# Three rotating diagonal slots, separate spreads of queries and values, and rows split into halves once per group and turned by transfers, in an attention and mixture-of-experts kernel

## The reference

```python
def xattn(q, k, v):                       # q = layernorm(x), k = v = ctx; each (4096, 16 heads, 16)
    scores = einsum('sqd,skd->sqk', qh, kh) / sqrt(16)
    scores = where(tril(ones(16, 16)), scores, -1e18)
    return einsum('sqk,skd->sqd', softmax(scores), vh)
...
def ffn(x, gate_w, gate_b, w1, b1, w2, b2):
    top1 = argmax(x @ gate_w.T + gate_b)
    for e in range(8):
        h = relu(x @ w1[e].T + b1[e])     # 1024 hidden
        y = h @ w2[e].T + b2[e]
        out = out + where(top1 == e, y, 0)
...
x = x + xattn(layernorm(x), ctx, ctx)
x = x + ffn(layernorm(x), ...)
```

## Time and profile before

| | |
|---|---|
| median of 3 runs | 477.7 us (477.31 to 478.84) |
| span of the profiled execution | 492.6 us |
| PE busy, share of the span | 402.1 us, 82% |
| DVE busy | 346.3 us, 70% |
| ACT busy | 177.5 us, 36% |
| POOL busy | 208.7 us, 42% |
| chain that ended last, by engine | PE 55%, DMA 11%, SPq 9%, DVE 9%, issue 6%, POOL 5% |
| bytes moved by DMA | 69.39 MB |

### The profile page before, as it was taken

One profiled execution on the slowest core, in us unless ns is written; L12 is line 12 of the kernel. 1 busy time (PEld: TensorE's weight loads), 2 busy tenths in 40 slices (PEclk: granted clock), 3 DMA queues, 4 the chain that ended last, 5 costly groups with the idle time before them and its releaser, 6 DMA issues.

```text
span 492.6 us, 16316 instructions
## 1 busy us (share of the span) xinstructions
PE 402.1 (82%) x5967; PEld 338.3 (69%) x5967; DVE 346.3 (70%) x777; ACT 177.5 (36%) x317; POOL 208.7 (42%) x213
## 2 busy tenths in 40 slices
PE   0135868888888866897999999779999999999992
PEld 0025757887787765896887877557778877877871
DVE  7978969789945863477757877457666666766662
ACT  3343255542624221342434433224333333433420
POOL 8345374334673467523723242642333323233221
PEclk9999999999999999975699999889999999999998
DMA  8999578899685664377612232544333322222210
GB/s 282 414 305 218 135 170 241 212 259 260 160 220 119 152 167 107 106 173 181 207 45 67 68 76 81 185 131 155 90 68 77 77 62 62 69 60 61 84 31 0
DMA packets 105162, 69.39 MB, mean 141 GB/s; under 512 B 78077, under 2 KB 88190, under 8 KB 104576
## 3 DMA queue, kind: packets, MB, share of 16 engines
q1 hardware_dynamic: 75696, 56.67, 41.9%
q10 hardware_dynamic: 25984, 3.21, 4.6%
q0 software_dynamic: 3408, 8.46, 4.6%
HBM read 48.28 MB, written 12.57 MB: 124 GB/s over the span
## 4 chain that ended last, share of the span: by engine, by line
PE 55%; DMA 11%; SPq 9%; DVE 9%; issue 6%; POOL 5%; ACT 2%; ACTq 1%; another core or an unknown queue 1%; POOLq 0%; DVEq 0%
PE s_ps L1229 20%; SPq L305 8%; PE at_ps L1245 6%; DMA arena<-qv_hl 6%; PE pv_ps L1245 6%; PE pv_ps L1143 6%; PE s_ps L1111 3%; PE lg_ps L1171 3%; PE pv_ps L1246 3%; PE at_ps L1246 3%; POOL qv_hl L987 2%; PE tr_ps L1156 2%; DMA arena<-x 2%; PE st_ps L1196 2%; POOL k_hl L995 1%
## 5 line engine op out<-in xcount | busy, mean ns | idle before, releaser
L1229 PEld LDWEIGHTS s_ps<-arena 128*128 x1872 | 132.7, 99 | 52.2 <-issue 14.6
L1229 PE MATMUL s_ps<-arena 128*128 128x128 f16 x1872 | 158.6, 222 | 8.4 <-DVE arena L906 5.1
L915 DVE SCALAR_TENSOR_TENSOR arena<-arena,s_ps 128x512 f32<-128x512 f32 x78 | 53.6, 687 | 48.6 <-PE s_ps L1229 35.9
L1076 POOL DMA_INDIRECT result<-arena x39 | 38.8, 995 | 95.5 <-DVE arena L940 91.6
L1111 PEld LDWEIGHTS s_ps<-k_hl,arena 128*128 128x128 f16 x1536 | 54.3, 118 | 29.9 <-DMA arena<-qv_hl 22.1
L1111 PE MATMUL s_ps<-k_hl,arena 128*128 128x16 f16 x1536 | 54.7, 179 | 23.3 <-DMA arena<-qv_hl 19.3
L1143 PE MATMUL pv_ps<-a_hl,arena 128*128 128x16 f16 x1536 | 54.7, 179 | 19.7 <-DMA arena<-qv_hl 15.9
L1143 PEld LDWEIGHTS pv_ps<-a_hl,arena 128*128 128x128 f16 x1536 | 53.5, 118 | 22.8 <-DMA arena<-qv_hl 18.3
L1245 PE MATMUL at_ps<-arena,k_in 128*128 x160 | 60.9, 383 | 0.8 <-DVE k_hl L926 0.6
L1245 PE MATMUL pv_ps<-arena,x_in 128*128 x152 | 58.1, 383 | 0.1
L1069 POOL TENSOR_TENSOR arena<-arena 128x256 f32<-128x256 f32 x39 | 30.7, 786 | 60.7 <-DMA arena<-b 60.6
(11 more groups left out here) (143 smaller groups left out, 614.2 us busy)
## 6 DMA issues: line engine op xcount, KB each, us to landing
arena<-w SPq DMA_DIRECT2D x28, 512.0 KB, 6.1
arena<-sorted_rows SPq DMA_DIRECT2D x39, 130.0 KB, 2.4
arena<-b SPq DMA_DIRECT2D x39, 128.0 KB
arena<-qv_hl SPq DMA_DIRECT2D x70, 64.0 KB, 3.5
k_in<-k_t SPq DMA_DIRECT2D x16, 256.0 KB, 3.9
v_in<-v_t SPq DMA_DIRECT2D x16, 256.0 KB
arena<-x SPq DMA_DIRECT2D x4, 1024.0 KB, 12.1
o_sb<-x_r SPq DMA_DIRECT2D x16, 256.0 KB, 3.8
```

Of the source, the lines that this page charges most:

```text
L915: eng.scalar_tensor_tensor(out=h_in[:, c].rearrange("p (k t) -> p k t", t=P), in0=bias, scalar=W_SCALE, in1=h_ps[c][:].rearrange("p (k t) ...
L1076: eng.indirect_dma_start(out=out, out_offset=bass.IndirectOffsetOnAxis(ap=rows[:, r, :].bitcast(I32)[:, D + 2:D + 3], axis=0), in_=rows[:, ...
L1229: k = eng.matmul(o, weights_of(j, w + k_ * H + n * P, P), xt[:, j % 2, k_ * P:(k_ + 1) * P], start=k_ == 0 and w is HI_1 and xt is xt_hi, ...
```

## The change

1. **Three slots in rotation.** Block i uses slot i mod 3 for its queries and, once its scores are done, for its values. `spread_first_part` and the joint transfer go; each block has eight parts of queries (waiting for outputs of block i-3) and eight of values (waiting for scores of block i), half as large as the joint ones. Expert 7's late load waits for outputs of block 14 (`s_pv >= NC - 1`); the first fetch of rows waits for outputs of block 13.
2. **Rows split per group.** After a group's layer norm, ScalarE normalises its rows (8 activations), casts them to fp16 (2 copies), and GpSimd subtracts for the rests (2 operations). Both halves travel in the row: 516 floats for 260. The scatter waits for them. In the expert stage a transposing transfer (`dma_start_transpose`) brings 128 rows x 512 halves into `xt`, three buffers; the plain fetch brings the first 260 floats. Normalisation, transposes and split per tile go on ScalarE, TensorE and VectorE, and with them the bank `st_ps` there. The residual add waits for the fetch.
3. **Zeros.** A lane of their own on GpSimd; VectorE clears the first slot.
4. **Order.** The due times of all lanes stand in a table `TIMES`, in hundredths of a microsecond, and all are new; ScalarE's three parts are steps of their own. Expert tiles are due 5.28 us apart from 338.87 us on.
5. The buffer of GpSimd's DMA descriptors is set to 4096 bytes.

```diff
-    ROW = D + 4
+    FETCHED = D + 4
+    ROW = FETCHED + D
...
-        q_bd = diagonals[:, 2 * SLOT_BLOCKS:], diagonals[:, 0:SLOT_BLOCKS]
-        v_bd = [q_bd[0] if i == NC - 2 else diagonals[:, SLOT_BLOCKS:2 * SLOT_BLOCKS] for i in range(NC)]
+        SIDES = 3
+        diagonal = [diagonals[:, n * SLOT_BLOCKS:(n + 1) * SLOT_BLOCKS] for n in (1, 2, 0)]
...
+        xn1 = sb("xn1", [P, G // 2, D])
+        x1_hi, x1_lo = [pay[:, :, FETCHED:].bitcast(F16)[:, :, n * D:(n + 1) * D] for n in range(2)]
...
-        def spread_part(eng, i, n):
+        def spread_part(eng, i, n, halves_of):
             part, cols = slice(HD * n, HD * (n + 1)), slice(HEADS * n, HEADS * (n + 1))
-            at = slice(1 - i % 2, 3 - i % 2)
-            if i + 2 < NC:
-                to = diagonals[part, at.start * SLOT_BLOCKS:at.stop * SLOT_BLOCKS, cols]
-                eng.dma_start(to, qv_hl[part, at].rearrange("p s b c u a -> p (s b) c u a")).then_inc(s_bd[i % 2], 16)
-            else:
-                eng.dma_start(v_bd[i][part, :, cols], v_hl[part]).then_inc(s_bd[i % 2], 16)
+            eng.dma_start(diagonal[i % SIDES][part, :, cols], halves_of[part]).then_inc(s_bd[i % SIDES], 16)
...
                     if e == E - 1:
-                        sp.wait_ge(s_qk, NC)
+                        sp.wait_ge(s_pv, NC - 1)
...
+            def spread_queries():
+                for i in range(NC):
+                    yield
+                    if i < SIDES:
+                        sp.wait_ge(*((s_zero_0, 1), (s_zero, 1), (s_zero, 2))[i])
+                    else:
+                        sp.wait_ge(s_pv, i - SIDES + 1)
                     sp.wait_ge(s_q_hi, i + 1)
                     sp.wait_ge(s_q_lo, i + 1)
+                    for n in range(8 - LATER):
+                        spread_part(eng, i, n, q_hl[i % 2])
+
+            def spread_values():
+                for i in range(NC):
+                    yield
                     sp.wait_ge(s_v_hi, i + 1)
                     sp.wait_ge(s_v_lo, i + 1)
+                    sp.wait_ge(s_qk, i + 1)
                     for n in range(8 - LATER):
+                        spread_part(eng, i, n, v_hl)
...
-                    sp.wait_ge(s_pv, NC - 1)
+                    sp.wait_ge(s_pv, NC - 2)
...
-                    eng.dma_start(rows[:, r, :], sorted_rows[bass.ds(row, P), :]).then_inc(s_rows[r], 16)
+                    if j >= XB:
+                        sp.wait_ge(s_up, 2 * (j - XB + 1))
+                    eng.dma_start_transpose(xt[:, j % XB], sorted_halves[bass.ds(row, P), 2 * FETCHED:]
+                                            ).then_inc(s_xt[j % XB], 16)
+                    eng.dma_start(rows[:, r, :], sorted_rows[bass.ds(row, P), 0:FETCHED]).then_inc(s_rows[r], 16)
...
-            def expert_inputs():
-                for j in range(NTILES):
-                    r = j % FR
-                    yield tile_at(j)
-                    act.wait_ge(s_rows[r], 16 * (j // FR + 1))
-                    act.wait_ge(s_xt2, j)
-                    eng.activation(xn2, rows[:, r, 0:D], ACT.Identity, scale=rows[:, r, D + 1:D + 2],
-                                   bias=rows[:, r, D:D + 1]).then_inc(s_xn2, 1)
-                    yield tile_at(j) + 1.5
-                    act.wait_ge(s_xt2, j + 1)
-                    act.wait_ge(s_up, 2 * (j - 1))
-                    eng.copy(xt_hi[:, j % 2], xt2_ps).then_inc(s_xt_hi, 1)
+            def normalised_rows():
+                for g in range(NG):
+                    for m in range(2):
+                        half = slice(m * G // 2, (m + 1) * G // 2)
+                        for b in range(half.start, half.stop):
+                            yield
+                            act.wait_ge(s_ln1, g + 1)
+                            act.wait_ge(s_x1_lo, 2 * g + m)
+                            eng.activation(xn1[:, b - half.start], pay[:, b, 0:D], ACT.Identity, scale=pay[:, b, D + 1:D + 2],
+                                           bias=pay[:, b, D:D + 1]).then_inc(s_xn1, 1)
+                        yield
+                        act.wait_ge(s_xn1, G * g + half.stop)
+                        eng.copy(x1_hi[:, half], xn1[:]).then_inc(s_x1_hi, 1)
...
+            def low_rows():
+                for g in range(NG):
+                    for m in range(2):
+                        half = slice(m * G // 2, (m + 1) * G // 2)
+                        yield
+                        pool.wait_ge(s_x1_hi, 2 * g + m + 1)
+                        eng.tensor_tensor(x1_lo[:, half], xn1[:], x1_hi[:, half], ALU.subtract).then_inc(s_x1_lo, 1)
...
+                        pool.wait_ge(s_x1_lo, 2 * g + 2)
...
-                    pool.wait_ge(s_xn2, j + 1)
+                    pool.wait_ge(s_rows[j % FR], 16 * (j // FR + 1))
...
-            def expert_inputs():
-                for j in range(NTILES):
-                    yield tile_at(j) + 0.6
-                    pe.wait_ge(s_q, NC)
-                    pe.wait_ge(s_xn2, j + 1)
-                    pe.wait_ge(s_xt_lo, j)
-                    for k_ in range(KD):
-                        k = eng.transpose(xt2_ps[:, k_ * P:(k_ + 1) * P], xn2[:, k_ * P:(k_ + 1) * P], ident[:])
-                    k.then_inc(s_xt2, 1)
...
-                            pe.wait_ge(s_xt_lo, j + 1)
-                            pe.wait_ge(s_xt_hi, j + 1)
+                            pe.wait_ge(s_xt[j % XB], 16 * (j // XB + 1))
...
-    nc = bacc.Bacc("TRN2", target_bir_lowering=False, num_devices=1)
+    nc = bacc.Bacc("TRN2", target_bir_lowering=False, num_devices=1, dynamic_dma_scratch_size=4096)
```

More of the change, by code:

```diff
@@ L210, in xattn_moe_kernel @@
         s_rows = [sem(f"s_rows{n}") for n in range(FR)]
+        s_xt = [sem(f"s_xt{n}") for n in range(XB)]
         s_b1, s_b2 = [[sem(f"{w}_{n}") for n in range(2)] for w in ("s_b1", "s_b2")]
@@ L244, in xattn_moe_kernel @@
         LATER = 3
-        TILE = 5.7
+        TILE = 5.3
         UNIT = TILE / KH
```

513 lines of the change are left out of this document (283 added, 230 removed), and 100 rows, old and new, of tables (TIMES, act, op1).

## The result

The changed kernel took 505.06 us (median of 4 runs, 500.86 to 507.42) where the kernel before took 478.27 us beside it (4 runs): a ratio of 1.053, 95% interval 1.047 to 1.059. That is slower by 26.8 us, where 9.4 us faster was forecast, and it lies outside the range of 453 to 487.

A forecast was written before the change was run, and what follows sets the result against it. Attention was read as a chain of waits, the expert tiles as TensorE's own work. Terms -8.6 - 4 + 3.2 + 0 = -9.4 us took 477.7 to 468.3 us, with a range of 453 to 487.

The forecast's parts named there:

- The loop through qv_hl: Attention: outputs end, SyncE issues spreads, they land, next outputs start; 10.8 us per block, of which TensorE works 3.4.
- the one on outputs of block 15: Attention's end: the prediction is wrong if outputs of block 15 end more than 8 us away from 238.
- The transposes off TensorE: Expert stage: input transposes leave TensorE, 39 tiles x 0.22 us, all on the path; -8.6 us.
- The replacements: Normalisation, casts and subtractions per group on ScalarE and GpSimd: last group covered by the choice of experts; 0, up to +12.5 uncovered.
- The transposing transfer: Expert tiles' row fetch: lands in 2.4 us (7.0 at the far bound), issued two tiles ahead; cost 0.
- The stall before tile 13: Four tiles from 299.52 to 331.90 us lose 10.4; part of it goes, -4 us, bounds -10.4 and +8.
- the fills hold the tiles: Rival, expert stage: doubled fill bytes bring the stall back and tile 17 comes 8 us late; 480.3 us, chance 0.12.
- The last expert's weights: End of attention: expert 7's load waits for block 14's outputs, not block 15's scores; +3.2 us, bounds 0 and +3.2.
- The diagonals: Attention: third slot ends the 10.8 us loop but 144 transfers become 256; taken as 0, bounds -15.9 and +33 us.
- SyncE becomes the bound of attention: Rival, attention: ten parts per block fill SyncE's issue time, +15 us, up to +33; 483.3 us, chance 0.18.
- Attention also gets shorter: Rival, attention: outputs' wait for spreads goes and the new order uses it, -15.9 us; 452.4 us, chance 0.15.
- The carry-over: Whole kernel: the profiled span's 14.9 us above the median of the runs was kept as a fixed difference.

The follow-up runs named there:

- x1_rows: Kernel before with only the rows' part: normalised split rows of 516 floats and the transposing transfer, attention as before; 517.32 us, 1.037 of before.
- x1b_rows: x1_rows with each group's normalisation moved to one stretch right behind the layer norm, ahead of the next weights; 501.81 us, 1.046 of before.
- x2_attention: Changed kernel with the expert stage and rows of before: three diagonals, 256 half-size spreads, new order on every engine; 517.88 us, 1.039 of before.
- b0_before: Kernel before, not edited, profiled again in the series where every kernel ran longer; 504.07 us.
- b0c_before: Kernel before, not edited, profiled in a later series as a run of the usual time; 479.86 us, span 478.1.
- b1b_ring: Kernel before with only the GpSimd descriptor scratch set to 4096 bytes, repeated on another chip; 476.37 us for 480.64, 0.991.
- b4_bytes: Kernel before with rows of 2064 bytes in scatters and fills (added half zeros, unread) and the 4096-byte scratch; 484.93 us, 1.007 of before.
- b2_cut: Kernel before with each joint spread cut in two, 256 transfers for 144, same place and waits, two diagonals; 502.56 us, 1.053 of before.
- x3_three: Three diagonals and 256 separate spreads, values first, but every engine in the order of before and rows as before; 1.024 of before.
- x4_share: x3_three with the eight parts of each spread shared 4 and 4 between SyncE and ScalarE, for 5 and 3; 493.14 us, 1.024 of before.
- b5_values: b2_cut with values' parts issued ahead of queries' parts and outputs waiting for values alone, two diagonals; 1.022 of before.
- a7_fills: Changed kernel with first fetches and tile 0's residual add put later, and the 12 fills issued by ScalarE instead of SyncE; 511.89 us.

## Why the prediction was wrong

*What bounds the kernel.* The loop through qv_hl was read rightly, and so was what follows it: the wait went, and softmax came in its place. But that reading stopped at the wait. Of the 10.8 us of a block, 4.2 were the issues themselves, and the change adds to just these. Of its own signs of being wrong, the one on outputs of block 15 came up first: they end at 256.5, 18 us away from 238.

*The transposes off TensorE, -8.6.* Right: the unit is 0.66 us, tiles are 5.28 apart with no gap, 38 x 0.22 = 8.4 us.

*The replacements, 0.* Right for the last group, which had been costed: the second subtraction ends at 323.5 (321.36 + 2.12), the row numbers come at 332.5. For groups 0 to 2 they stand amid attention, and the 23 us of ScalarE were counted and then taken at nothing. x1_rows and x1b_rows put 22 to 25 us on the rows' part alone, in two orders. Beside the new attention it costs far less: first ups are 25.3 us late in x2_attention and 29.0 in the whole change, each against its own profile of before.

*The transposing transfer, 0.* Right that it sets no pace: the steady stretch has no gap. It costs SyncE 1.23 us to issue, which the prediction didn't count, and lands in 3.8 us (median), between the 2.4 taken and the 7.0 of the far bound. The Trainium skill's figure (VectorE: DVE Perf Modes, The three transpose paths and the rules behind it) came to an estimated 5.2 us; the trace's median is under it. The lines:

```profile
L641 SPq DMA_TRANSPOSE arena<-sorted_rows x39: 1217/1230/1955, 235.8 to 480.8; - x39
...
DMA to landing us min/median/max: 2.7/3.8/5.7
```

*The stall before tile 13, -4.* Wrong in sign and in its base. The 10.4 us of the earlier trace rows are not in every run: b0_before has them (32.0 us for these four tiles), but b0c_before loses 2.4 there (24.40 for 22.0) and b1b_ring 1.3, so in a run of the usual time there was little to win. The fills' bytes, given a bound of +8, cost about 8 us by b4_bytes against b1b_ring. So the rival "the fills hold the tiles" had the mechanism and the size of the bytes. What it did not have is that x2_attention takes 38.15 us for the tiles 12 to 15 without these bytes.

*The last expert's weights, +3.2.* The step itself was right: the load is issued at 251.49, on the end of block 14's outputs (251.46), and the first ups follow 13.5 us later. It costs nothing, as block 15's outputs at 253.12 and the gates are later.

*The diagonals, 0 (bounds -15.9 and +33).* This is the term that failed. Attention's part alone (x2_attention) puts first ups 25.3 us later; the cut into 256 transfers alone (b2_cut) puts outputs' end 21.4 us later. With values first and three diagonals it is 17.0 (x3_three); the rest is the new order's, five us of it the gate matmuls ahead of the first ups. Its own arithmetic had +34 us of issues on SyncE and +19 on ScalarE, and the medians give 160 x 0.614 - (70 x 0.744 + 18 x 0.61) = +35. The prediction put 0 between the bounds because both sides had nearly full engines. It should have gone well up towards the upper one: one side was a wait that could only shrink to the next wait, the other was work on two queues that every wait of the loop passes through. That last reason is argued from the chains, not tested by itself.

*What had no term.* The scratch (item 5) gave 3.5 us at the end. The new order (item 4) took 2 to 9 us of attention, the gate matmuls apart, and is enough for the stall at the tiles 12 to 15.

*The rivals.* "SyncE becomes the bound of attention" (0.18, 483.3, +33 at its end) comes nearest; b2_cut measured +21.4. It was right that the added issues cost attention some 20 us. As a picture of the changed kernel it is only in part so: SyncE still waits 32 us for keys and values to be split (20.7 + 8.0 + 3.4, for 24.6 + 16.1 in b0c_before), and one part per block taken off it (x4_share) gained nothing. "Attention also gets shorter" (0.15) is refuted by b5_values against x3_three: the loop it would have opened gives nothing.

*The carry-over.* The difference of 14.9 us between span and median was carried over as a constant. It was no constant but a longer run, and it hid that tiles of a run of the usual time are 5.66 and not 5.70 apart and that its stall is small.

*The range.* The two slow sides, attention and tiles, could fall together, and did (+29 at first ups, 12.9 in the tiles 9 to 16). The range took in half of one.

## What to carry to other kernels

Count transfers, not bytes, wherever an in-order queue both issues them and serves the work around them: splitting a transfer to free a dependency costs one more issue on every turn of the loop, and this must be set against the wait it removes before anything else. Compare the span of a profile with the median of the runs first, and where they differ by more than a few us, trust no stall of that profile as typical.

When bytes are added to a burst, look at what small transfers are issued in it: issuing the burst faster made those land later. And when a change brings a new order of all engines, price the order as a term of its own: here x2_attention had the stall that would else be put down to bytes and to SyncE.

## What the runs showed of the hardware

- Issuing a strided transfer of 64 KB takes SyncE 0.74 us (b0c_before), one of 32 KB 0.61 (b2_cut); in the changed kernel a plain fetch takes 0.43 and a transposing one 1.23. At a DMA share of 1.1 the transposing issue rose to 6.2 us (346.69 in a7_fills).
- The transfer engines gave 307 to 335 GB/s at a share of 1.07 to 1.10 (a7_fills); a 128 KB transposing fetch issued in it landed after 20.1 us, for 3.8 in the median of the changed kernel.
- TensorE's granted clock is at its lower level (1.2 GHz) from 112 to about 270 us in the changed kernel, mean 0.69 in attention for 0.85 before, after a stretch with TensorE busy 60.0 of 87 us. It shows in no group of attention: 96 matmuls of 128x16 took 3.32 us at 75.31, at 2.4 GHz, and 3.33 at 253.12, at 1.2 GHz, and 32 gate matmuls took 7.03 us at 1.2 GHz where 16 took 3.56 at 2.4 (96.58). What it slows is the first tile, whose 48 ups take 4.85 us, nearly all at this level, for 8 x 0.34 = 2.7 at 2.4 GHz.
- A scratch of 4096 bytes for GpSimd's descriptors shortens the last DRAIN of GpSimd's queue from 7.07 to 3.56 us, and made before 1.2% and 0.9% faster in two series.
